# A two-layer graph network on one core: the setup rewritten around the edge records, and the pairs of tiles shifted by a place

## The chip, the cores and the metric

The kernel runs on one core of one Trainium2 chip. The metric is device time in microseconds (us), the median of several runs; "the profile" is one further execution recorded by the hardware profiler. The engines are TensorE (PE in the rows; PEld is its weight load), VectorE (DVE), ScalarE (ACT), GpSimd (POOL) and SyncE (SP), which only issues transfers. Transfers are issued by SP, ACT and POOL, each of which executes its program strictly in order.

## The reference, cut to what matters

```python
h = relu(layernorm(x))                                    # x: 1250 nodes x 512
weight = einsum('rb,bio->rio', w_comp, bases)             # 32 relations from 8 bases
msg = einsum('ni,rio->rno', h, weight)[etype, src] * edge_weight   # 40000 edges
x = x + segment_sum(msg, dst) + h_bias
h = relu(layernorm(x))
h = h @ W.T + b
row, col = edges and self loops; dis = rsqrt(degree)
x = x + relu(segment_sum(dis[row] * dis[col] * h[row], col))
```

The edges come sorted by destination (`dst`), and the low node numbers have far more of them than the high ones.

## The kernel before, in words

**Tiles and slots.** The nodes fall into 20 tiles of 64. Two tiles make a pair (ten pairs); `PAIR` says which, `PORDER` in which order the pairs are worked on. Each tile has a fixed number of slots of 128 edges, 335 in all. For every slot POOL gathers 128 rows of the table of normalised features (`rows_layer0`, 2,304 bytes a row) into one of eight buffers (`gath`, L766), and PE multiplies them with a one-hot matrix scaled by the edge's eight basis values (`sel`): twelve matmuls (L1614) sum the rows into the tile's accumulator, and one more (L1620) counts the edges by source for layer 1. L1620 is the last matmul of a slot, so its rows are the clock of the slots. DVE makes `sel` four slots at a time (L1194 to L1200).

**Ends of tiles.** When a tile's last slot is done, ACT and DVE split the accumulator into two halves of 16 bits (`flush`: ACT L874, DVE L1278, then the counts, DVE L1284 to L1287 and ACT L877). PE cannot begin the next tile's sums before that. When both tiles of a pair are done, 96 matmuls ("products", L1636) multiply them with the bases, which ACT and DVE have split likewise, one of eight bases at a time (`split_base`: ACT L885, DVE L1347). A planner (`place_products`) spreads the products over the slots behind; they are written into the order of PE. In the last stretch "partial" matmuls (L1643) of layer 1 take their place.

**Steps.** `STEPS[s]` lists what else each engine does at slot s: `flush`, `bsplit` (a base), `types`/`look` (the values of eight edge slots: one-hot of the relation by DVE L1140 from `types`, a matmul by PE L1514, the sum by DVE L1147, a cast by ACT L826), `largest`/`scale` (the scales of the bases and W, for which ACT must have squared all eight bases and W, L841).

**Setup.** SP loads the edge arrays and `x`; ACT packs source, destination, relation and weight of each edge into a record and writes the records to memory (L793 to L800). DVE and PE count the edges of each tile (L991, L1481, L1016 to L1024), which gives each slot its first edge. POOL then gathers the records slot by slot (`padr`, L738), and PE turns them so that an edge's fields stand in columns (L1496 to L1501); from these come `srcs`, the relations (`types_by_slot`, written out by SP L630 and loaded again by L624), and a `flag` that says whether the edges are in order. Meanwhile DVE takes the mean and variance of each 128 rows of `x` (L1008), ACT normalises them (L818) and casts them to the high half (L814), and the low half is made by POOL for seven of ten (L745) and by DVE for three (L1057). SP writes both halves into the table (L639). POOL waits for the whole table, the flag and `srcs` before the first gather; from the sixth gather on also for `s_cols`, which DVE gives when the column codes stand (L1180).

**What SP has in its queue**, in order: the identity blocks of the table (L607), a copy of `x` out of SBUF to `x_base` (L612), bases 0 to 4, the relations, the table, `types` 0 to 2, bases 5 to 7, the biases, W (L671), `types` 3 to 5, and two blocks of `x_base` back (L668).

## Time and profile before

| | before |
|---|---|
| median of 3 runs | 617.85 us (615.9 to 618.54) |
| the profiled execution | 612.81 us |
| its span, first to last instruction | 611.0 us |
| granted TensorE clock, mean | 0.909 |
| PE busy | 491.6 us of the span |
| POOL busy | 358.1 us |
| DVE busy | 347.5 us |
| ACT busy | 152.3 us |
| moved by the DMA engines | 132.32 MB |

A busy time is the sum of an engine's instructions; the granted clock is a share of full speed, and TensorE has two levels, 1.2 and 2.4 GHz (0.50 and 1.00 in the rows). The difference of 1.8 us between span and execution lies around the instructions.

### The profile page before, as it was taken

How to read it: one execution, taken by the hardware profiler on the slowest of the kernel's cores; microseconds unless marked ns; L12 is line 12 of the kernel's file. 1: busy time of each engine (PE TensorE's matmuls, PEld its weight loads, DVE VectorE, ACT ScalarE, POOL GpSimd, SP SyncE). 2: the span in 40 equal slices, each digit the busy share in tenths (PEclk: the TensorE clock that was granted, in tenths of full speed). 3: DMA queues.
4: the chain of work that ended last, by engine and by line, in shares of the span. 5: the costliest groups of instructions: out<-in, count | busy, mean ns of one | idle time of the engine just before them, and what ended most of it. 6: DMA issues, size and time to landing. Idle time of an engine off the chain costs nothing.

```text
span 611.0 us, 16039 instructions
## 1 busy us (share of the span) xinstructions
PE 491.6 (80%) x5902; PEld 313.8 (51%) x5902; DVE 347.5 (57%) x971; ACT 152.3 (25%) x272; POOL 358.1 (59%) x473
## 2 busy tenths in 40 slices
PE   3031446397999999999999999998999999989984
PEld 1021435265666666665565556555555565555531
DVE  7798137976575435755554754788646543332045
ACT  3392224552232011222220220320313202123010
POOL 3333626876676776775765757768747777760000
PEclk9655655699999999999999999998999999999986
DMA  8896965557786887795884867856867877773106
GB/s 281 295 351 225 392 187 145 160 160 201 221 273 202 243 271 225 215 277 176 251 254 144 273 208 221 273 179 189 268 178 212 255 238 237 239 231 107 33 11 162
DMA packets 53109, 132.32 MB, mean 217 GB/s; under 512 B 12109, under 2 KB 18110, under 8 KB 53030
## 3 DMA queue, kind: packets, MB, share of 16 engines
q0 software_dynamic: 27040, 99.60, 53.7%
q1 hardware_dynamic: 25036, 30.47, 16.0%
q8 instruction: 58, 0.95, 0.6%
q10 hardware_dynamic: 954, 1.13, 0.6%
q14 instruction: 21, 0.17, 0.1%
HBM read 120.32 MB, written 10.84 MB: 215 GB/s over the span
## 4 chain that ended last, share of the span: by engine, by line
PE 53%; DVE 13%; DMA 12%; issue 8%; ACT 5%; POOL 4%; SPq 3%; ACTq 1%; DVEq 0%
PE PS L1636 24%; PE PS L1614 17%; DMA gath<-rows_layer,srcs 7%; PE PS L1643 5%; PE PS L1684 4%; POOL gath L766 4%; DMA types<-types_by_slot 2%; SPq L624 2%; DVE room_b L1278 2%; ACT room_b L885 2%; DVE zt L1278 1%; DMA edge_records<-room_c 1%; DMA w1t<-edge_records,w1t 1%; DVE room_b L1347 1%; PE PS L1620 1%
## 5 line engine op out<-in xcount | busy, mean ns | idle before, releaser
L766 POOL DMA_INDIRECT gath<-rows_layer,srcs x335 | 341.8, 1020 | 168.8 <-issue 86.7
L1614 PE MATMUL PS<-sel,gath 128*128 128x48 f16 (+7 forms) x4020 | 315.7, 206 | 40.4 <-DVE zt L1278 12.1
L1614 PEld LDWEIGHTS PS<-sel,gath 128*128 128x128 f16 x4020 | 245.5, 102 | 164.6 <-issue 71.7
L1636 PE MATMUL PS<-room_b,zt 128*128 128x512 f16 x480 | 163.8, 385 | 1.4 <-DVE sel L1200 1.4
L1636 PE MATMUL PS<-room_b 128*128 128x512 f16 (+1 forms) x480 | 151.1, 380 | 0.9 <-DMA gath<-rows_layer,srcs 0.4
L1620 PE MATMUL PS<-oh_ad,gath 128*128 128x30 bf16 (+7 forms) x335 | 64.7, 193 | 0.0
L1194 DVE TENSOR_TENSOR masks<-iota_n,dloc 128x24 bf16<-128x24 f32 (+12 forms) x92 | 17.9, 195 | 80.9 <-issue 44.5
L1643 PE MATMUL PS<-u_t,room_c 128*128 128x512 f16 (+2 forms) x180 | 57.5, 404 | 3.7 <-issue 2.1
L1636 PEld LDWEIGHTS PS<-room_b 128*128 128x128 f16 (+1 forms) x480 | 47.3, 104 | 14.8 <-DVE room_b L1278 0.6
L826 ACT CAST val<-val_f 128x64 f16<-128x64 f32 x42 | 11.0, 261 | 168.4 <-DVE val_f L1151 163.4
L1636 PEld LDWEIGHTS PS<-room_b,zt 128*128 128x128 f16 x480 | 45.1, 99 | 5.9 <-issue 1.5
L1200 DVE TENSOR_TENSOR sel<-masks,val 128x192 f32<-128x192 bf16 (+12 forms) x92 | 38.8, 422 | 0.0
L1620 PEld LDWEIGHTS PS<-oh_ad,gath 128*128 128x128 bf16 x335 | 34.4, 103 | 3.1 <-issue 2.6
L1278 DVE SCALAR_TENSOR_TENSOR room_b<-PS,room_b 128x512 f16<-128x512 f32 x40 | 24.8, 683 | 13.5 <-ACT room_b L874 13.4
L1514 PE MATMUL PS<-wparts,oh_t 128*128 128x96 bf16 x84 | 10.8, 212 | 26.6 <-DVE oh_t L1140 24.6
L1278 DVE SCALAR_TENSOR_TENSOR zt<-PS,zt 128x512 f16<-128x512 f32 x40 | 24.8, 683 | 10.5 <-ACT zt L874 10.5
L1196 DVE TENSOR_TENSOR oh_ad<-iota_n,code 128x120 bf16<-128x120 f32 (+12 forms) x92 | 29.7, 323 | 0.0
L1147 DVE TENSOR_REDUCE val_f<-PS 128x64 f32<-128x192 f32 x42 | 14.9, 356 | 25.3 <-PE PS L1514 24.6
L1684 PE MATMUL PS<-w1t,hT_t 128*128 128x512 f16 (+1 forms) x120 | 27.5, 379 | 1.0 <-DVE val_f L1147 1.0
L877 ACT CAST room_c<-c_i 128x320 f16<-128x320 int32 (+1 forms) x40 | 16.1, 450 | 47.1 <-DVE c_i L1287 47.1
L1643 PEld LDWEIGHTS PS<-u_t,room_c 128*128 128x128 f16 (+2 forms) x180 | 18.4, 105 | 15.6 <-issue 8.1
L874 ACT ACTIVATE zt<-PS 128x512 f16<-128x512 f32 x40 | 20.6, 601 | 18.5 <-PE PS L1620 18.5
(227 smaller groups left out, 436.4 us busy)
## 6 DMA issues: line engine op xcount, KB each, us to landing
room_b<-in_L_gnn_bases_dram SPq DMA_DIRECT2D x8, 1024.0 KB, 9.9
gath<-rows_layer,srcs POOLq DMA_INDIRECT x335
types<-types_by_slot SPq DMA_DIRECT2D x168, 16.0 KB
x_t<-x_base SPq DMA_DIRECT2D x19, 128.0 KB, 5.0
u_t<-in_x_dram SPq DMA_DIRECT2D x9, 256.0 KB, 6.2
x_base<-u_t SPq DMA_DIRECT2D x9, 256.0 KB
x_layer<-x_t SPq DMA_DIRECT2D x16, 128.0 KB, 4.1
gath<-x_layer SPq DMA_DIRECT2D x16, 128.0 KB, 2.8
```

Source lines behind the costliest of these rows:

```text
L766: pool.indirect_dma_start(out=gath[:, s % UN, :], out_offset=None, in_=tab0_d[:, :], in_offset=bass.IndirectOffsetOnAxis(ap=srcs[:, s:s + ...
L874: a.activation(zt[q % 2][:, 0, f, :, TN * h:TN * (h + 1)], zbank(f), ACT.Copy, scale=ZDOWN).then_inc(s_hi, 1)
L877: a.copy(C[:, HA * k:HA * (k + 1), at:at + n], c_i[:, k, :].rearrange("p (a d) -> p a d", d=TN)[:, :, 0:n]).then_inc(s_cst, 1)
L1194: v.tensor_tensor(mask, iota_n[:, 0:w].unsqueeze(1).to_broadcast([P, k, w]), dloc[:, s:s + k].unsqueeze(2).to_broadcast([P, k, w]), ALU.is ...
L1196: v.tensor_tensor(oh_ad[:, there, 0:k, 0:HA * w], iota_n[:, 0:HA * w].unsqueeze(1).to_broadcast([P, k, HA * w]), code[:, s:s + k].unsqueez ...
L1200: v.tensor_tensor(sel[:, there, 0:k, 0:NB * w].rearrange("p k (b d) -> p k b d", b=NB), mask.unsqueeze(2).to_broadcast([P, k, NB, w]), val ...
L1278: v.scalar_tensor_tensor(lo, zbank(f), ZDOWN, hi, ALU.mult, ALU.subtract).then_inc(s_lo, 1)
L1614: mm(there, gath[:, s % UN, D * t + P * f:D * t + P * (f + 1)], sel_parts[:, here, k, 0:NB * w, u], start=first and t == 0 and u == 1, sto ...
L1620: mm(there, oh_r[:, s % UN, :], oh_ad[:, here, k, 0:HA * w], start=first, stop=True, skip_group_check=True).then_inc(s_used, 1)
L1636: last = mm(PS[0:r, PBANK[q], :], zt[q % 2][:, t, f, b, 0:r], base_hl[:, b, u, f, :], start=(m == 0), stop=(m == NM - 1))
L1643: return mm(PS[0:r, bank, :], there, u_part(i, t)[0:ROWS[i], :], start=start, stop=True, skip_group_check=not start)
L1684: last = mm(PS[0:r, MB, :], hT_t[:, s, f, 0:r], w1t[:, t, f, :], start=(f == s == t == 0), stop=(f == FT - 1 and s == 1))
```

## The change

It does these things.

- **Pairs.** `PAIR` is shifted by a place and `PORDER` is new: the first pair is now tiles 18 and 19 (9 and 5 slots; it was tiles 9 and 10 with 13 and 12), the last one tiles 0 and 17 (73 and 9; it was 0 and 19 with 73 and 5). The codes of the columns cost two more DVE instructions of 128x336. The bases are split at steps 9, 11, ... 23 (they were at 10, 13, ... 31), and the planner may place products from slot 24 on (it was 26). The identity blocks now come in four kinds instead of two (eight small DVE instructions instead of four, four writes instead of three).
- **SP.** The copy of `x` to `x_base` goes from memory to memory, in four transfers, behind the biases. The identity blocks wait for the record gather. `types` 3 to 5 stand right behind `types` 0 to 2. W is loaded again late, since the first load may be overwritten on another path.
- **ACT.** It issues bases 5 to 7 and a first load of W itself, behind the normalisation; it squares W before the first slot instead of at step 3. It normalises `x` in two groups of five.
- **POOL.** It makes no low halves any more; DVE makes all ten.
- **DVE.** It gives the standard deviation in two groups; behind the records it makes three low halves, then `srcs`, the checks and the flag, then the seven others, then the small table of `w_comp`.
- **PE.** The counting runs in four groups of five tiles (64 matmuls of 100 columns instead of 16 of 400), and the turned local index comes first.

```diff
-    PORDER = [5, 4, 6, 9, 3, 7, 2, 8, 1, 0]
-    PAIR = [(2 * p, NTI - 1 - 2 * p) for p in range(NT)]
+    PORDER = [9, 3, 4, 5, 6, 2, 7, 1, 8, 0]
+    TURN = NT - 2
+    PAIR = [(2 * p, 2 * ((TURN - p) % NT) + 1) for p in range(NT)]
...
-        SQ_SETUP, SC_AT, BS_AT, WT_AT = BEARLY, 7, 10, 38
+        SQ_SETUP, SC_AT, BS_AT, WT_AT = BEARLY, 7, 9, 38
...
-            STEPS[BS_AT + 3 * n].append(("bsplit", n))
+            STEPS[BS_AT + 2 * n].append(("bsplit", n))
...
-            GATHER, LAND, FREE, READY, RESERVE, FIRST = 5.8, 12.0, 14.0, 15.0, 14, 26
+            GATHER, LAND, FREE, READY, RESERVE, FIRST = 5.8, 12.0, 14.0, 15.0, 14, 24
...
-            for i in range(NT):
-                sp.wait_ge(s_xin[i], 16)
-                sp.dma_start(xbase_d[P * i:P * i + XROWS[i], :], x_in[0:XROWS[i], i, :]).then_inc(s_xbase, 16)
+            sp.wait_ge(s_rec_out, 48)
             load_base(0)
             sp.wait_ge(s_padr, 16 * C0)
+            sp.wait_ge(s_ident_fac, 2 * len(KINDS))
...
-            for v in range(1, TRING):
+            for v in range(1, TRING + VEARLY):
                 load_types(v)
-            for n in range(BEARLY, NB):
-                load_base(n)
...
+            for lo, hi in ((0, TN * HA), (TN * HA, P * HA), (P * HA, P * (NT - 2)), (P * (NT - 2), N)):
+                sp.dma_start(xbase_d[lo:hi, :], x[lo:hi, :]).then_inc(s_xbase, 16)
...
+            sp.wait_ge(s_sqb, SQ_SETUP + 1)
             sp.dma_start(w_in, W1.rearrange("(c p) i -> p c i", p=P)).then_inc(s_win, 16)
-            sp.wait_ge(s_xbase, 16 * NT)
-            for v in range(TRING, TRING + VEARLY):
-                load_types(v)
+            sp.wait_ge(s_xbase, 64)
             load_x(0)
             load_x(1)
...
-            for i in range(LOWS):
-                pool.wait_ge(s_h0hi, i + 1)
-                t = table_of(i)
-                g.tensor_tensor(t[:, 1, :], x_in[0:XROWS[i], i, :], t[:, 0, :], ALU.subtract).then_inc(s_h0lo_pool, 1)
...
+            for n in range(BEARLY, NB):
+                act.dma_start(base_in[:, n + 2, :, :], bases[n, :, :].rearrange("(f p) o -> p f o", p=P)).then_inc(s_bin[n], 16)
+            act.wait_ge(s_h0lo, FT)
+            act.dma_start(w_in, W1.rearrange("(c p) i -> p c i", p=P)).then_inc(s_win, 16)
             act.wait_ge(s_sqt, 1)
             for n in range(SQ_SETUP):
                 squares_of(n)
             for v in range(VEARLY):
                 val_hi(v)
+            squares_of(NB)
...
             for i in range(2, NT):
                 moments0(i)
+                if i == GROUP0:
+                    deviation(0)
...
-            pe.wait_ge(s_ohlt, NTI)
+            for r in range(0, NTI, CNT):
+                pe.wait_ge(s_ohlt, r + CNT)
+                for j in range(EC // 20):
+                    last = mm(PS[:, 0, 20 * r:20 * (r + CNT)], ones_b[0:EP, :], oh_lt[:, r:r + CNT, 20 * j:20 * (j + 1)],
+                              start=(j == 0), stop=(j == EC // 20 - 1))
```

How the order moves is seen at three places. First SP's queue from the last table write on, before; `room_b` holds the bases, `u_t` the rows of x and later W.

```order
L639 DMA rows_layer<-room_c 98x1024 [waits s_h0lo]
L624 DMA types<-types_by_slot 32x256 x8
L603 DMA room_b<-in_L_gnn_bases_dram 128x4x512 x3
L645 DMA hb_t<-in_L_gnn_h_bias_dram 128x512
L646 DMA b_t<-in_L_gnn_b_dram 128x512
...
L671 DMA u_t<-in_L_gnn_W_dram 128x4x512 [waits s_tab0]
L624 DMA types<-types_by_slot 32x256 [waits s_oht,s_xbase]
L624 DMA types<-types_by_slot 32x256 x3
```

The same stretch of SP's queue after the change.

```order
L645 DMA rows_layer<-room_c 98x1024 [waits s_h0lo]
L633 DMA types<-types_by_slot 32x256 x8
L633 DMA types<-types_by_slot 32x256 [waits s_oht]
L633 DMA types<-types_by_slot 32x256 x3
...
L649 DMA hb_t<-in_L_gnn_h_bias_dram 128x512
L650 DMA b_t<-in_L_gnn_b_dram 128x512
L652 DMA x_base<-in_x_dram 16x10240 x2
L652 DMA x_base<-in_x_dram 16x12288
L652 DMA x_base<-in_x_dram 16x7232
...
L678 DMA u_t<-in_L_gnn_W_dram 128x4x512 [waits s_sqb,s_tab0]
L674 DMA x_t<-x_base 64x512 [waits s_xbase]
```

The loads of `types` 3 (and, in the rows left out, 4 and 5) no longer stand behind the four loads of 1 MB, and the block of `x_base` that comes back stands behind a copy from memory to memory.

Second, DVE in the setup, before, from the sources (`srcs`) to the first scale (`bound`); `room_c` and `zt` hold the table's halves, `gath` is scratch here.

```order
L1102 CAST srcs<-PS 128x336 [waits s_tr]
...
L1125 COPY wtT<-PS 128x336 [waits s_tr,s_link]
...
L1130 TENSOR_SCALAR flag<-gath 1x1 [waits s_link]
L1057 TENSOR_TENSOR room_c<-u_t,room_c 128x512 [waits s_h0hi] x2
L1057 TENSOR_TENSOR room_c<-u_t,room_c 98x512 [waits s_h0hi]
L1112 TENSOR_SCALAR bound<-bound 128x1
```

The same part of DVE's order after the change.

```order
L1064 TENSOR_TENSOR zt<-u_t,zt 128x512 [waits s_h0hi] x3
L1100 COPY gath<-PS 128x336 [waits s_tr]
...
L1116 CAST srcs<-PS 128x336 [waits s_tr]
...
L1125 TENSOR_SCALAR flag<-gath 1x1 [waits s_link]
L1064 TENSOR_TENSOR zt<-u_t,zt 128x512 [waits s_h0hi] x2
L1064 TENSOR_TENSOR room_c<-u_t,room_c 128x512 [waits s_h0hi] x4
L1064 TENSOR_TENSOR room_c<-u_t,room_c 98x512 [waits s_h0hi]
L1130 TENSOR_SCALAR zt<-zt 128x1
```

DVE has ten low halves instead of three, three of them ahead of `srcs` and seven behind the flag.

Third, DVE at the end of the first tile, before: the scales (`unscale_x` is their last), a base (`room_b<-room_b,scale_i`), the flush (`zt<-PS,zt`).

```order
L1341 TENSOR_SCALAR unscale_x<-unscale_i 128x1 [waits s_link]
L1140 TENSOR_SCALAR oh_t<-types,rel 128x256 [waits s_look,s_types1,s_scaled]
L1347 SCALAR_TENSOR_TENSOR room_b<-room_b,scale_i 128x2048 [waits s_bhi]
L1194 TENSOR_TENSOR masks<-iota_n,dloc 128x4x11 [waits s_sel,s_used,s_val]
L1196 TENSOR_TENSOR oh_ad<-iota_n,code 128x4x55
L1200 TENSOR_TENSOR sel<-masks,val 128x4x88 [waits s_mask]
L1278 SCALAR_TENSOR_TENSOR zt<-PS,zt 128x8x64 [waits s_hi] x4
```

The same place after the change, from the first tile's flush to the second tile's.

```order
L1310 SCALAR_TENSOR_TENSOR zt<-PS,zt 128x8x64 [waits s_hi] x4
...
L1374 TENSOR_SCALAR unscale_x<-unscale_i 128x1 [waits s_link]
L1380 SCALAR_TENSOR_TENSOR room_b<-room_b,scale_i 128x2048 [waits s_bhi,s_scaled]
L1169 TENSOR_SCALAR oh_t<-types,rel 128x256 [waits s_look,s_types1]
L1327 TENSOR_TENSOR room_c<-room_c,ident 128x64 [waits s_cst]
L1333 TENSOR_REDUCE deg_p<-room_c 128x10 [waits s_own]
L1335 TENSOR_TENSOR deg<-deg,deg_p 128x10 [waits s_degp]
L1380 SCALAR_TENSOR_TENSOR room_b<-room_b,scale_i 128x2048 [waits s_bhi]
...
L1310 SCALAR_TENSOR_TENSOR zt<-PS,zt 128x8x64 [waits s_hi] x4
```

The first flush now stands ahead of the scales, and two bases stand ahead of the second one, which ends a tile of five slots.

## Rows read from the trace of the kernel before

**Rows 1.** The page, busy time of each engine: us, share, instructions.

```profile
PE 491.6 (80%) x5902; PEld 313.8 (51%) x5902; DVE 347.5 (57%) x971; ACT 152.3 (25%) x272; POOL 358.1 (59%) x473
```

**Rows 2.** Busy time by stretch; last: granted clock, DMA share, GB/s.

```profile
57.00:78.00 21.00, 6.48 (x91) 6.19 (x91) 5.89 (x20) 6.27 (x7) 13.13 (x13) 0.58 1.03 387
72.10:84.98 12.88, 0.00 (x0) 0.03 (x1) 0.43 (x4) 3.17 (x3) 1.89 (x2) 0.56 0.95 294
86.00:140.00 54.00, 36.84 (x458) 27.99 (x456) 43.36 (x90) 23.98 (x28) 40.37 (x29) 0.70 0.54 154
500.00:545.00 45.00, 41.71 (x620) 26.31 (x619) 13.59 (x49) 7.21 (x13) 34.11 (x36) 1.00 0.79 238
```

**Rows 3.** Chain that ended last, in order of time: start, length, what.

```profile
11.19 7.42 DMA edge_records<-room_c
...
21.55 7.31 DMA w1t<-edge_records,w1t
...
60.53 7.05 SPq L624
...
69.94 14.58 DMA types<-types_by_slot
...
538.82 4.60 DMA gath<-rows_layer,srcs
...
558.71 20.92 PE PS L1636 x96
```

**Rows 4.** Timeline of POOL: start, length, line, idle before.

```profile
28.23 6.04 POOL L745 TENSOR_TENSOR zt<-u_t,zt 128x512 f16<-128x512 f32 x5 [5.73 <-ACT zt L814]
...
54.59 0.96 POOL L766 DMA_INDIRECT gath<-rows_layer,srcs  x1 [17.87 <-issue]
...
61.37 1.04 POOL L766 DMA_INDIRECT gath<-rows_layer,srcs  x1 [0.30 <-issue]
...
93.60 2.69 POOL L766 DMA_INDIRECT gath<-rows_layer,srcs  x1 [0.30 <-issue]
```

**Rows 5.** Timeline of DVE in the setup.

```profile
28.95 0.46 DVE L1043 COPY w1t<-w1t 128x3 f32<-128x3 f32 x1 [2.61 <-DMA w1t<-edge_records,w1t]
...
29.51 1.12 DVE L1045 TENSOR_SCALAR w1t<-w1t 128x3 f32<-128x3 f32 x1
30.66 0.16 DVE L1046 TENSOR_TENSOR w1t<-w1t 128x3 f32<-128x3 f32 x1
...
33.10 3.75 DVE L1050 TENSOR_SCALAR w1t<-w1t 128x128 f32<-128x128 f32 x3
...
48.58 1.87 DVE L1057 TENSOR_TENSOR room_c<-u_t,room_c 128x512 f16<-128x512 f32 x3
...
60.72 0.20 DVE L1194 TENSOR_TENSOR masks<-iota_n,dloc 128x40 bf16<-128x40 f32 x1
```

**Rows 6.** Timeline of SP: transfers issued.

```profile
10.49 9.10 SPq L612 DMA_DIRECT2D x_base<-u_t  x10
```

**Rows 7.** Timeline of PE: first slot, then ends of slots 24, 28, 48, 252, 334.

```profile
64.61 0.98 PE L1614 MATMUL PS<-sel,gath 128*128 128x80 f16 x12 [7.76 <-issue]
...
113.22 0.26 PE L1620 MATMUL PS<-oh_ad,gath 128*128 128x55 bf16 x1
...
125.41 0.19 PE L1620 MATMUL PS<-oh_ad,gath 128*128 128x50 bf16 x1
...
156.17 0.20 PE L1620 MATMUL PS<-oh_ad,gath 128*128 128x55 bf16 x1
...
446.04 0.20 PE L1620 MATMUL PS<-oh_ad,gath 128*128 128x65 bf16 x1
...
554.92 0.20 PE L1620 MATMUL PS<-oh_ad,gath 128*128 128x65 bf16 x1
```

**Rows 8.** Waits of PE up to 145 us: total, times, longest.

```profile
PE PS L1514 <- DVE oh_t L1140: 24.6, 5, 12.9
```

**Rows 9.** DVE's half of the split of a base, all eight.

```profile
L1347 DVE SCALAR_TENSOR_TENSOR room_b<-room_b,scale_i x8: 2344/2350/2352, 93.1 to 133.1; 128x2048 f16<-128x2048 f32 x8
```

More of the change, by code:

```diff
@@ L229, in gnn_kernel @@
         gap_max = take_g(f32, SL)[0:1, :]
-        assert all(TROWS[i] == TN for i in TORDER[:-1])
         rec = rec_w[0:EP, :].rearrange("p (c k) -> p c k", k=4)
@@ L1027, in _ @@
                 moments0(i)
+                if i == GROUP0:
+                    deviation(0)
             v.memset(stats[:, :], 0.0).then_inc(s_stat0, 1)
@@ L1074, in _ @@
             v.reduce_sum(viol_s, viol, AX.X)
+            low(0)
+            low(1)
+            low(2)
+            dve.wait_ge(s_tr, 1)
+            link(v.tensor_copy(dloc_f, PS[:, 1, 0:SLV]))
+            link(v.tensor_tensor(valid, dloc_f, win_c, ALU.is_lt))
+            link(v.reduce_sum(have, valid[:, 0:SL], AX.X))
+            v.tensor_scalar(have, have, -float(E) / P, None, ALU.add).then_inc(s_have, 1)
+            dve.wait_ge(s_slotmm, 1)
+            link(v.tensor_copy(row_f, PS[0:1, PB, 0:SLP]))
+            v.tensor_tensor(same[:, 0:NSAME], row_f[:, REP:SL], row_f[:, 0:NSAME], ALU.is_equal)
+            begin = PS[0:1, CB, 0:SL + 1]
+            dve.wait_ge(s_gap, 1)
+            v.tensor_copy(hops[:, SL:SL + 1], begin[:, 0:1])
+            link(v.tensor_tensor(hops[:, 0:SL], begin[:, 1:SL + 1], gap_max, ALU.subtract))
+            link(v.tensor_tensor(hops[:, 0:SL], hops[:, 0:SL], begin[:, 0:SL], ALU.is_gt))
+            v.reduce_sum(bad, same[:, 0:NSAME + SL + 1], AX.X).then_inc(s_have, 1)
+            dve.wait_ge(s_tr, 2)
+            v.tensor_copy(srcs[:, :], PS[:, 2, 0:SLV]).then_inc(s_srcs, 1)
+            begins = PS[0:1, CB, 0:SLP].rearrange("p (g k) -> p g k", k=WPACK)
+            link(v.tensor_copy(pack_f, begins[:, :, WPACK - 1]))
+            for k in reversed(range(WPACK - 1)):
+                there = pack_f if k else slots[0:1, :]
+                link(v.scalar_tensor_tensor(there, pack_f, float(1 << WBITS), begins[:, :, k], ALU.mult, ALU.add))
+            dve.wait_ge(s_okmm, 1)
+            link(v.tensor_scalar(ok3, PS[:, 0, 0:3], 0.0, None, ALU.is_equal))
+            link(v.tensor_reduce(ok, ok3, AX.X, ALU.min))
+            v.tensor_scalar(flag[0:1, :], ok[0:1, :], -1.0, 1.0, ALU.mult, ALU.add).then_inc(s_flag, 1)
+            for i in range(3, NT):
+                low(i)
+            link(v.tensor_scalar(blk_i, part_i, R.bit_length() - 1, None, ALU.logical_shift_right))
+            link(v.tensor_copy(blk, blk_i))
             link(v.scalar_tensor_tensor(rel[:, :], blk, -float(R), part_f[:, :], ALU.mult, ALU.add))
@@ L1126, in _ @@
             link(v.tensor_tensor(bound[:, SC_V:SC_V + 1], sq_max[:, :], sq_max[:, :], ALU.mult))
-            dve.wait_ge(s_okmm, 1)
-            link(v.tensor_scalar(ok3, PS[:, 0, 0:3], 0.0, None, ALU.is_equal))
-            link(v.tensor_reduce(ok, ok3, AX.X, ALU.min))
-            v.tensor_scalar(flag[0:1, :], ok[0:1, :], -1.0, 1.0, ALU.mult, ALU.add).then_inc(s_flag, 1)
-            for i in range(LOWS, NT):
-                low(i)
             powers(SC_V, SC_V + 1)
@@ L1493, in _ @@
             columns_of(0)
-            pe.wait_ge(s_loc, 2 * C0)
+            pe.wait_ge(s_loc, C0)
+            for c in range(C0):
+                last = tr(PS[:, 1, P * c:P * (c + 1)], padr[:, c, :, 1], ident[:, :])
+            last.then_inc(s_tr, 1)
             for c in range(C0):
```

149 lines of the change are left out of this document (74 added, 75 removed).

## The prediction

> **What bounds the kernel now.** I read the busy times first. PE is busy for 491.6 of 611.0 us and no other engine comes near [rows 1], so PE bounds the kernel as a whole; what it does not work, it waits, and where it waits is read from the chain that ended last and from the ends of the slots. The first slot begins at 64.61 us [rows 7]: the setup is a tenth of the time, and PE has almost nothing to do in it. From 72.10 to 84.98 PE does nothing at all [rows 2]. The longest wait of PE up to 145 us, 12.9 us, is for the one-hot of the relations [rows 8], and the chain says why: SP stood 7.05 us in the issue of a `types` load and the load then took 14.58 us to land [rows 3]. It stood behind three bases and W, 4 MB, in SP's own queue, while the DMA engines were full (share 1.03, 387 GB/s from 57 to 78 us [rows 2]). From 86 to 140 us DVE is the engine that sets the pace, 43.36 of 54.00 us busy against PE's 36.84, at a mean granted clock of 0.70 [rows 2]. After that PE is nearly always busy, until the last stretch: from 500 to 545 us POOL makes 36 gathers, one per 1.25 us (45.00 / 36), and PE follows them [rows 2]. The chain ends with 96 products in 20.92 us, 0.218 us each [rows 3].
>
> **The setup, step by step.** Without the `x_base` copy, which SP issued from 10.49 to 19.6 us [rows 6], the writing of the records (7.42 us) and their gather (7.31 us) [rows 3] have the DMA engines almost to themselves; the nearest undisturbed transfer takes 4.60 us to land [rows 3], so the records can be there between 23 us and the present 28.86. It makes little difference: DVE stood waiting only 2.61 us for them, so it was free at 26.34 [rows 5]. The extra identity blocks fall into its wait for the counting, and the second half of the deviation may cost it 0.3 us: it begins at about 26.6 instead of 28.95.
>
> Then comes the part that POOL slows. While POOL subtracts (28.23 on, seven instructions [rows 4]), DVE's 128x3 instructions take 1.12 us, and 0.16 us where they miss one; the three of 128x128 take 3.75 us [rows 5]. Seven such instructions would take about 2.5 us instead of 8: with POOL's share gone, the columns and relations are out 8 us earlier, at about 29.2. This pays for the work that DVE takes over: seven low halves at 0.62 us (1.87 / 3 [rows 5]) are 4.4 us, three of ten ahead of `srcs`, the rest behind the flag. The last low half then ends at about 43.6, where now it ends at 50.45 [rows 5]; SP writes the table until 45 to 46, now beside bases 5 to 7 and W on ACT's queue. At 387 GB/s [rows 2] these 4.2 MB are 10.8 us of the DMA engines, of which the table may meet half. First gather: 47 at best, 54.6 as now [rows 4] at worst; I take 50.5. DVE's chain to the first `masks`, now at 60.72 [rows 5], gains 4 us in scales and low halves and loses about 1 for the two new code instructions and 1 for `types` 1, which land behind the table: 58 to 60. PE began 3 to 4 us behind `masks` [rows 5, 7]; I take 60.5 for the first slot instead of 64.6: **-4.1** (bounds 0 and -8).
>
> **The hole.** `types` 3 is issued right behind `types` 2, at about 49 us, on a queue without the 1 MB loads. Even 14.58 us to land [rows 3] would bring it at 64, before slot 6 needs it (60.5 plus 7 slots of 1.07 us, from 64.61 to 72.10 [rows 2, 7], is 68). **-12.9.**
>
> **What is late next.** Slots 7 to 28 took from 84.98 to 125.60 [rows 2, 7], 40.6 us, paced by DVE. The same DVE work waits there now, closer together: the second tile has five slots, so its flush comes behind the scales and two bases of 2.35 us [rows 9] (each behind ACT's half), and `look` 5 at slot 22 behind three more. Queued behind these on DVE are the selections and the flush that PE needs. At best the stretch keeps its 40.6 us; at worst it takes 5.9 us more, since now all eight bases have to be split before the flush at slot 28, where five or six of them had been (2.5 x 2.35). The wait behind two bases at slot 13 is the nearest thing, but PE has slots in hand at slot 22; I take **+1.9**. Slot 28 then ends at 110.5: 125.6 - 4.1 - 12.9 + 1.9.
>
> **From slot 28 to 48.** 30.8 us now (125.60 to 156.37 [rows 7]). Counted in the order, PE has 82 products there instead of 57: 25 x 0.218 = +5.5. The bases that are done by then no longer stand in DVE's way (up to -5.9); I take half: **+2.5**.
>
> **From slot 48 to 252.** The same 13 tile ends and 655 products instead of 657; the columns of the edges up to slot 252 are the same in sum, counted from the windows: **0**. The other order of the tiles changes which slots are narrow, not their sum; I allow 4 us to both sides.
>
> **From slot 252 to 334.** 108.9 us now (446.24 to 555.12 [rows 7]). 29 products are no longer in it, 6.3 us where PE bounds, nothing where POOL's 1.25 us a gather do. More than half of it is of the second kind [rows 2]: **-1.9**. The tail behind slot 334 is the same work: 96 products, the last partial sums, the output.
>
> **Sum.** -4.1 - 12.9 + 1.9 + 2.5 - 1.9 = -14.5. The profiled execution took 612.81 us (span 611.0); it would take 598.3. The median of the runs is 617.85, 5 us above the profiled one; from it the forecast is 603.4 us.
>
> **The rivals.**
>
> *The gathers are held up* (10%). Between 80 and 112 us the eight bases fill DVE for 18.8 us. A gather that met a base took 2.69 us instead of 0.95 [rows 4], 1.74 us more; if each base costs PE that much, 14 us are lost. Against it speaks that the eight buffers hide a single late gather, and that 29 gathers in 54 us lost only 0.44 us each to it (40.37 / 29 - 0.95 [rows 2]). Half of the 14 gives -7.5: 610 us. The Trainium skill (SBUF — State Buffer, section "SBUF: two separate sides") says that DVE and GpSimd share a pair of ports as an exclusive lock, held for the whole instruction, the loser fully blocked. By that rule every base blocks POOL for its full length and the sum would be near -7.5 or less; the rows on POOL's subtractions bear the lock out, those on the gathers only in part.
>
> *The hole stays* (5%). The change would not do what it says if `types` 3 were late for another reason than SP's queue, say because the DMA engines are as full as before: the copy of `x` (2.56 MB), the second W and the biases now run from 55 to 70. The 12.9 us stay and the gain is 1.6: 616 us. Against it: SP itself stood still for 7.05 us [rows 3], which only its own queue explains. The Trainium skill (Trainium Kernel Development and Optimization, section "Key Constraints") says that issuing from several engines saves only the sequencer's issue time, since all queues run on the same 16 DMA engines. By it the move of four loads to ACT's queue would be worth the 7.05 us of issue and not the landing, and the sum would be about -8; no row of the kernel before shows two queues with large loads at once.
>
> *Slower* (5%). `types` 6, which DVE needs at slot 25 (about 105 us), now stands in SP's queue behind the first block of `x_base`, and that behind a copy from memory to memory of which the trace shows no example. The nearest row issues 2.5 MB in 9.1 us [rows 6]; issued at 56 it would be there before 75. If the copy ran at a sixth of 387 GB/s and landed at 95, nothing would be lost; from about 97 on each us is one of PE's, and beyond 112 the kernel is slower than before. Landing at 120: 626 us.
>
> *More than forecast* (5%): the start at -8 and the last stretch at -6.3, 594 us.
>
> **Chances and range.** The forecast, a gain of 8 to 20 us, holds 75%; the four rivals 25%. A difference within 0.5%, 3.1 us, is about what a measurement of this kernel cannot tell from none. Faster: the forecast, the held gathers, the larger gain: 0.89; the same: 0.06; slower: 0.05. The range of 596 to 612 reaches from the larger gain into the held gathers.
>
> **What would show it.** Right: the first slot at 59 to 62 us; DVE's instructions of 128x3 at 0.2 us throughout; no wait of PE above 8 us behind the first slot; a wait at slot 14 for DVE (flush behind two bases) of 4 to 8 us; slot 28 at 108 to 113; slot 252 at 430 to 437; the stretch from 500 us on paced by gathers of 1.25 us. Wrong: a first gather that still waits until 54 us, PE waiting for `types` or for ACT's squares at slots 6 and 7, or an SP that stands at the second block of `x_base`.

## The result, and the profile after

| | before | after |
|---|---|---|
| median, same chip | 616.88 us (614.38 to 618.54, 4 runs) | 627.98 us (627.2 to 630.05, 4 runs) |
| ratio to before | | 1.021 (95% interval 1.0174 to 1.0246) |
| the profiled execution, its span | 612.81, 611.0 us | 627.2, 625.4 us |
| PE busy | 491.6 us | 488.8 us |

The change makes the kernel 2.1% slower; forecast were 603.4 us and a gain. (Ratios here and below are taken over undisturbed runs alone, so they are not quite those of the medians, here 1.018.) The two profiled executions stand 14.4 us apart, the medians 11.1: the one of before was faster than any of its four timed runs, so the distances to before by slot, which are read from the traces, may be some 3 us too large. The page of the changed kernel first, busy time of each engine, answering to [rows 1].

```profile
PE 488.8 (78%) x5954; PEld 313.2 (50%) x5954; DVE 347.3 (56%) x989; ACT 153.0 (24%) x273; POOL 353.5 (57%) x466
```

PE works 2.8 us less in a span that is 14.4 us longer: PE waits 17.2 us more. The question is where. The timeline of PE after, first slot and ends of slots 7, 28, 48, 252 and 334, answers to [rows 7]; L1657 is now the last matmul of a slot.

```profile
67.37 1.30 PE L1651 MATMUL PS<-sel,gath 128*128 128x104 f16 x12 [6.87 <-DVE sel L1231]
...
81.82 0.20 PE L1657 MATMUL PS<-oh_ad,gath 128*128 128x65 bf16 x1
...
124.60 0.20 PE L1657 MATMUL PS<-oh_ad,gath 128*128 128x45 bf16 x1
...
164.98 0.19 PE L1657 MATMUL PS<-oh_ad,gath 128*128 128x50 bf16 x1
...
463.78 0.19 PE L1657 MATMUL PS<-oh_ad,gath 128*128 128x60 bf16 x1
...
569.67 0.20 PE L1657 MATMUL PS<-oh_ad,gath 128*128 128x65 bf16 x1
```

The first slot begins 2.8 us later than before, behind a wait of 6.87 us that the profile puts down to DVE's `sel`. From slot 7 to 13 the change is ahead (82.0 against 86.3 at slot 7, by 4.3 us); at slot 28 it is ahead by 0.8, at 48 behind by 8.8, at 252 by 17.8, at the last slot by 14.8.

**The setup** got what was hoped for on DVE and lost it in the transfers. DVE's timeline after: an instruction of 128x3, the local indices, `srcs`, the last low halves.

```profile
26.05 0.17 DVE L1081 TENSOR_SCALAR w1t<-w1t 128x3 f32<-128x3 f32 x1
...
26.85 0.83 DVE L1086 TENSOR_SCALAR w1t<-w1t 128x128 f32<-128x128 f32 x3
...
35.84 0.48 DVE L1116 CAST srcs<-PS 128x336 uint32<-128x336 f32 x1
...
39.01 3.08 DVE L1064 TENSOR_TENSOR room_c<-u_t,room_c 128x512 f16<-128x512 f32 x5
```

The three instructions of 128x128 take 0.83 us where they took 3.75 [rows 5], and the last low half ends at 42.1 instead of 50.45. Now the chain that ended last, in this stretch, and the busy times by stretch (sum, then engines, granted clock, DMA share, GB/s).

```profile
31.50 12.95 DMA types_by_slot<-h_t
44.47 0.32 SPq L633
...
48.71 0.48 SPq L645
...
50.65 7.00 DMA types<-types_by_slot
...
65.48 13.12 DMA gath<-rows_layer,srcs
```

```profile
28.00:40.00 12.00, 6.31 (x29) 4.15 (x28) 11.52 (x31) 6.29 (x10) 0.00 (x0) 0.64 1.03 384
40.00:57.00 17.00, 0.32 (x2) 0.14 (x2) 7.81 (x33) 9.30 (x11) 0.00 (x0) 0.50 1.04 390
57.00:69.00 12.00, 2.26 (x23) 1.91 (x24) 9.41 (x31) 6.32 (x8) 7.71 (x8) 0.50 0.70 217
69.00:83.00 14.00, 8.27 (x105) 7.49 (x102) 2.69 (x11) 2.36 (x5) 7.02 (x9) 0.69 0.97 357
```

From 28 to 57 us the DMA engines are full: 29 us at 384 to 390 GB/s are 11.2 MB, seven bases and W (8 MB) among them. The 96 KB of relations, which SP issued behind bases 1 to 4 in its own queue, take 12.95 us to land. SP waits for them before it goes on to `types` 0 and the last six table writes (L645), so the last of these is issued at 48.71, 6.6 us behind the last low half. Then the sixth gather takes 13.12 us, beside the copy to `x_base` and the second W: a new hole where the old one was. `types` 1, issued behind the table at 50.65, landed 7.00 us later, and DVE's chain to the first `masks` (65.26) starts there. POOL's first and sixth gather, which stood at 54.59 and 61.37 [rows 4]:

```profile
58.62 0.95 POOL L766 DMA_INDIRECT gath<-rows_layer,srcs  x1 [37.44 <-issue]
...
65.48 1.15 POOL L766 DMA_INDIRECT gath<-rows_layer,srcs  x1 [0.84 <-DVE code L1211]
```

**Behind the setup**, from slot 8 to 29, PE has three long waits for DVE: for the flush at slot 13, for the one-hot of `look` 5 at slot 22, and for the flush at slot 28.

```profile
99.80 0.78 PE L1651 MATMUL PS<-sel,gath 128*128 128x72 f16 x6 [8.13 <-DVE zt L1310]
...
116.42 0.32 PE L1551 MATMUL PS<-wparts,oh_t 128*128 128x96 bf16 x2 [7.47 <-DVE oh_t L1169]
...
129.22 0.42 PE L1651 MATMUL PS<-sel,gath 128*128 128x88 f16 x3 [3.10 <-DVE room_b L1310]
```

The wait for the same look in the kernel before:

```profile
111.08 0.32 PE L1514 MATMUL PS<-wparts,oh_t 128*128 128x96 bf16 x2 [3.81 <-DVE oh_t L1140]
```

### The profile page after: what moved, and what is told of

It reads as the page before. It is cut to its first block, busy times and chain, and to the rows that moved or that the text cites. A ratio compares the mean times of both kernels' runs of the same rounds, so it can differ in the third digit from the quotient of the medians.

```text
span 625.4 us, 16152 instructions
## 1 busy us (share of the span) xinstructions
PE 488.8 (78%) x5954; PEld 313.2 (50%) x5954; DVE 347.3 (56%) x989; ACT 153.0 (24%) x273; POOL 353.5 (57%) x466
## 4 chain that ended last, share of the span: by engine, by line
PE 51%; DMA 17%; DVE 14%; issue 7%; ACT 4%; POOL 3%; SPq 2%; DVEq 0%; ACTq 0%; POOLq 0%
PE PS L1673 24%; PE PS L1651 17%; DMA gath<-rows_layer,srcs 13%; PE PS L1721 5%; PE PS L1680 4%; POOL gath L766 3%; DVE zt L1310 2%; DMA types_by_slot<-h_t 2%; ACT room_b L896 1%; DVE room_b L1380 1%; DMA types<-types_by_slot 1%; DVE room_b L1310 1%; PE PS L1657 1%; ACT zt L885 1%; DVE sel L1231 1%
## 5 line engine op out<-in xcount | busy, mean ns | idle before, releaser
L1673 PE MATMUL PS<-room_b,zt 128*128 128x512 f16 (+1 forms) x480 | 164.6, 387 | 1.1 <-DMA gath<-rows_layer,srcs 0.6
L1673 PE MATMUL PS<-room_b 128*128 128x512 f16 x480 | 150.7, 380 | 0.6 <-DMA gath<-rows_layer,srcs 0.6
L1657 PE MATMUL PS<-oh_ad,gath 128*128 128x30 bf16 (+7 forms) x335 | 64.3, 192 | 0.1
L1225 DVE TENSOR_TENSOR masks<-iota_n,dloc 128x24 bf16<-128x24 f32 (+12 forms) x92 | 17.8, 194 | 78.9 <-issue 45.2
L1680 PE MATMUL PS<-u_t,room_c 128*128 128x512 f16 (+1 forms) x180 | 55.6, 380 | 4.9 <-issue 3.3
L1673 PEld LDWEIGHTS PS<-room_b 128*128 128x128 f16 x480 | 44.7, 98 | 16.8 <-DMA gath<-rows_layer,srcs 0.7
L1673 PEld LDWEIGHTS PS<-room_b,zt 128*128 128x128 f16 (+1 forms) x480 | 48.0, 106 | 5.7 <-DMA gath<-rows_layer,srcs 0.7
L1657 PEld LDWEIGHTS PS<-oh_ad,gath 128*128 128x128 bf16 x335 | 34.0, 102 | 3.2 <-issue 2.2
L1551 PE MATMUL PS<-wparts,oh_t 128*128 128x96 bf16 x84 | 10.7, 210 | 31.6 <-DVE oh_t L1169 30.1
L1721 PE MATMUL PS<-w1t,hT_t 128*128 128x512 f16 (+1 forms) x120 | 29.7, 401 | 4.6 <-DVE val_f L1176 4.4
L885 ACT ACTIVATE room_b<-PS 128x512 f16<-128x512 f32 x40 | 20.6, 602 | 31.9 <-PE PS L1657 29.3
```

Source lines behind the costliest of these rows:

```text
L885: a.activation(zt[q % 2][:, 0, f, :, TN * h:TN * (h + 1)], zbank(f), ACT.Copy, scale=ZDOWN).then_inc(s_hi, 1)
L1225: v.tensor_tensor(mask, iota_n[:, 0:w].unsqueeze(1).to_broadcast([P, k, w]), dloc[:, s:s + k].unsqueeze(2).to_broadcast([P, k, w]), ALU.is ...
L1657: mm(there, oh_r[:, s % UN, :], oh_ad[:, here, k, 0:HA * w], start=first, stop=True, skip_group_check=True).then_inc(s_used, 1)
L1673: last = mm(PS[0:r, PBANK[q], :], zt[q % 2][:, t, f, b, 0:r], base_hl[:, b, u, f, :], start=(m == 0), stop=(m == NM - 1))
L1680: return mm(PS[0:r, bank, :], there, u_part(i, t)[0:ROWS[i], :], start=start, stop=True, skip_group_check=not start)
L1721: last = mm(PS[0:r, MB, :], hT_t[:, s, f, 0:r], w1t[:, t, f, :], start=(f == s == t == 0), stop=(f == FT - 1 and s == 1))
```

## The experiments

Two theories stood against each other for the loss: **the setup** (its transfers), and **the pairs** (tile ends, base splits and products lie elsewhere). All times of before in these runs are 614.6 to 615.2 us; ratios are to before on the same chip. Ends of slots, in us, read from each trace as above:

| slot | before | after | 1: old pairs | 2: new pairs alone | 4: copy late | 7: short pair fourth | 8: 1 and 4 | 10: splits late |
|---|---|---|---|---|---|---|---|---|
| 0 | 65.6 | 68.7 | 67.6 | 66.7 | 68.2 | 68.0 | 67.5 | 69.5 |
| 7 | 86.3 | 82.0 | 82.2 | 86.2 | 73.8 | 82.7 | 73.5 | 82.9 |
| 14 | 100.7 | 102.0 | 96.2 | 106.5 | 94.0 | 92.8 | 87.8 | 96.6 |
| 29 | 126.8 | 133.1 | 122.1 | 138.4 | 125.2 | 120.1 | 117.1 | 131.5 |
| 48 | 156.4 | 165.2 | 151.9 | 172.0 | 157.3 | 159.2 | 147.1 | 163.6 |
| 104 | 228.6 | 245.2 | 223.8 | 252.5 | 237.4 | 248.6 | 220.4 | 243.6 |
| 144 | 289.6 | 310.1 | 285.2 | 316.8 | 302.0 | 313.2 | 283.5 | 308.5 |
| 252 | 446.2 | 464.0 | 442.1 | 470.7 | 456.2 | 466.3 | 440.4 | 463.4 |
| 334 | 555.1 | 569.9 | 550.6 | 576.2 | 564.6 | 573.5 | 549.6 | 570.9 |

**1. The new setup with the old pairs.**

```diff
-    PORDER = [9, 3, 4, 5, 6, 2, 7, 1, 8, 0]
-    TURN = NT - 2
+    PORDER = [5, 4, 6, 9, 3, 7, 2, 8, 1, 0]
+    TURN = NT - 1
...
+        SQ_SETUP, SC_AT, BS_AT, WT_AT = BEARLY, 7, 10, 38
+            STEPS[BS_AT + 3 * n].append(("bsplit", n))
```

> The new setup with the old pairs, the old steps of the base splits (10, 13, 16, ...), the old first slot of products (26) and the old step of the histogram's preparation. Theory A (the loss is made by the pairs: products drawn 31 ahead at slot 48, flushes and splits closer together on DVE): the first slot ends near 68.7 us as in the changed kernel, slot 7 near 82 (4 ahead of before), and that lead is kept to the end: 610 to 614 us. Rival B (the loss is made by the setup's DMA traffic): the same late gathers and nothing won later: 624 to 628 us.

609.8 us, ratio 0.9925 (0.990 to 0.9949): a gain of 0.75%. It is 4.1 us ahead at slot 7 and 4.5 at the last slot. Theory A holds.

**2. The old setup with the new pairs**, the same lines the other way round.

> The old setup with the new pairs and all that goes with them (four kinds of identity, the split steps 9, 11, 13, ..., first product slot 24). Theory A (pairs cost): the hole at 74 to 87 us stays, and slots 8 to 48 cost some 10 us more on top: 626 to 632 us. Rival B (setup costs): about the time of before, 615 to 619 us.

635.96 us, ratio 1.0353 (1.0309 to 1.0398). Level with before at slot 7, 5.8 us behind at 14, 15.6 at 48, 27.2 at 144, 21.1 at the end. The pairs cost more than the 10 us of theory A. The setup is worth a gain, the pairs a loss some four times as large.

**3. The relations ahead of the identities and bases 1 to 4.**

```diff
+            sp.wait_ge(s_loc, 2 * C0)
+            for c in range(C0):
+                sp.dma_start(types_d[P * c:P * (c + 1), :], typ16[:, c, :]).then_inc(s_typd, 16)
             sp.wait_ge(s_ident_fac, 2 * len(KINDS))
```

> The changed kernel, with the three writes of the type rows issued ahead of the identities and of bases 1 to 4 on SP. Theory A (the type rows wait for the bases in SP's DMA queue and the table writes stand behind that on SP): the write lands in about 5 us instead of 13, types 0 near 44 instead of 51, the first gather is issued near 54 instead of 58.6, the first slot ends near 64, and the time falls by 3 to 5 us to 623 to 625. Rival B (the DMA engines are full until 56 us whatever the order): the write lands sooner but the table later or as late, first gather 57 to 59, time 626 to 629.

632.99 us, ratio 1.0297 (1.025 to 1.0344), slower than both theories said. Transfers of the two kernels, after and then here: issue, KB each, median us to landing.

```profile
types_by_slot<-h_t SPq DMA_DIRECT2D x3, 32.0 KB, 13.0
```

```profile
types_by_slot<-h_t SPq DMA_DIRECT2D x3, 32.0 KB, 1.6
```

The relations land in 1.6 us instead of 13.0, so it was the loads ahead of them. (In the changed kernel base 4 lands at 42.07 and the first of the relations at 42.80, which speaks for their place in SP's queue; but here they were issued while no other load was under way, so full engines are not ruled out.) But now the identities and bases are issued 5.7 us later (the bases from 31.64 instead of 25.90), the table's writes stand behind them, and the first gather comes at 64.32 instead of 58.62. The 96 KB themselves are not what delays the rest: SP now stands until DVE has the relations (it issues them at 28.25) before it goes on to identities and bases. A wait moved ahead in a queue delays all that is behind it.

**4. The copy to `x_base` and the second W later.** The copy, W and the first two loads of `x` back move from ahead of slot 0 to step 25 of SP's list.

```diff
+            for s in range(VEND):
+                if s == 25:
+                    with sp.If(any_order < 1):
+                        for lo, hi in ((0, TN * HA), (TN * HA, P * HA), (P * HA, P * (NT - 2)), (P * (NT - 2), N)):
+                            sp.dma_start(xbase_d[lo:hi, :], x[lo:hi, :]).then_inc(s_xbase, 16)
...
+                    load_x(0)
+                    load_x(1)
```

> The changed kernel, with the copy of x to x_base, the second load of W and the first two loads of x issued at step 25 of SP's list (behind the load of type rows 8) instead of ahead of slot 0. Theory A (the sixth gather took 13.1 us because the copy and the weight were in the queues beside it): gathers 6 to 8 land in 4 to 6 us, slot 4 ends near 73 instead of 78, and 3 to 5 us stay to the end: 623 to 625. Rival B (DVE's chain of looks and selections is late at slots 5 to 14 anyway, so an earlier gather only waits): slot 4 earlier, slot 14 as before, 626 to 629. Rival C (the moved copy now meets the gathers of slots 20 to 28): 629 to 633.

621.02 us, ratio 1.0107 (1.006 to 1.0153). Slot 4 ends at 71.6 instead of 78.2, slot 7 at 73.8 instead of 82.0, and 8 us of it stay until slot 252, 5.3 to the last. The busy times by stretch of this run show why:

```profile
69.00:83.00 14.00, 12.03 (x159) 10.56 (x157) 9.39 (x36) 6.17 (x10) 10.58 (x12) 0.74 0.83 245
```

PE does 12.03 us of work from 69 to 83 where the changed kernel did 8.27, and the DMA engines are no longer full. Theory A holds, with more than it asked for. Which of the copy, W and the loads back counts most was not separated.

**5 and 6. The products cut, with the new and with the old pairs.** After the first of each pair, a product takes 64 columns instead of 512.

```diff
-                    last = mm(PS[0:r, PBANK[q], :], zt[q % 2][:, t, f, b, 0:r], base_hl[:, b, u, f, :], start=(m == 0), stop=(m == NM - 1))
+                    w = D if m == 0 else 64
+                    last = mm(PS[0:r, PBANK[q], 0:w], zt[q % 2][:, t, f, b, 0:r], base_hl[:, b, u, f, 0:w], start=(m == 0), stop=(m == NM - 1))
```

> The changed kernel with every product but the first of each pair cut from 512 to 64 columns (left out: 7/8 of the products' computation). It is to be read against the same cut on the new setup with the old pairs. Theory P (the pairs cost by the order of the products: 31 to 60 more are drawn by slots 48 to 144 than with the old pairs, where PE is the bound, and they are missing as filler later, where the gathers are): with the products nearly free, the distance between the two kernels falls from 17.5 us to 8 or less by the last slot. Rival F (the pairs cost by DVE's flushes, splits and looks, which stand closer together): the distance stays at 15 to 20 us, as the waits for DVE don't depend on the products.

> The new setup with the old pairs, and the same cut of the products to 64 columns (left out: 7/8 of the products' computation). Theory P: 8 us or less faster than the cut kernel with the new pairs. Rival F: 15 to 20 us faster than it.

583.94 and 572.71 us: 11.2 us apart (17.5 with whole products, 2.85% of 615). In the traces the two stand 10.7 us apart at slot 29 and 10.8 at the last. With whole products it was 11.1 and 19.3. So the 8.2 us that the pairs lose behind slot 29 go with the products, and the 11 ahead of it don't. Neither theory alone: the loss has two halves. (From slot 29 on the granted clock of the two cut kernels was 0.81 and 0.82, of the whole ones 0.99 and 1.00, so the cut ones are compared with each other alone.)

Both halves are seen in the busy times by slots. Old pairs on the new setup, slots 9 to 14, 49 to 84, 185 to 252:

```profile
82.93:96.24 13.31, 6.24 (x83) 4.82 (x84) 10.59 (x32) 4.98 (x8) 8.31 (x7) 0.73 0.84 259
...
151.94:200.07 48.13, 45.88 (x604) 29.80 (x603) 28.96 (x85) 11.30 (x25) 33.32 (x36) 1.00 0.77 233
...
341.37:442.10 100.73, 92.76 (x1233) 59.96 (x1232) 65.40 (x187) 18.32 (x41) 72.92 (x70) 0.98 0.75 223
```

The changed kernel, the same slots:

```profile
83.08:102.02 18.94, 7.92 (x82) 6.23 (x82) 16.27 (x42) 8.72 (x12) 8.32 (x7) 0.72 0.68 202
...
165.17:218.24 53.07, 51.66 (x631) 32.85 (x629) 32.80 (x92) 12.88 (x28) 35.84 (x37) 1.00 0.78 230
...
365.11:463.97 98.86, 86.67 (x1216) 56.44 (x1213) 58.87 (x170) 14.03 (x32) 72.70 (x68) 1.00 0.75 219
```

In slots 9 to 14 DVE has 16.27 us to do instead of 10.59 (two flushes and two splits where the old pairs have one of each; the scales stand in both), and the stretch is 5.6 us longer. From slot 49 to 84 PE has 5.8 us more to do (23 products more, 5.0 us at 0.218) and the stretch is 4.9 us longer. From 185 to 252 it has 6.1 us less to do, and the stretch is only 1.9 us shorter: with fewer products PE waits there, 12.2 instead of 8.0 us. (17 products fewer are 3.7 of the 6.1 us; what else is in it, run 1's granted clock of 0.98 or the width of the slots, was not separated.) From the end of slot 29 to the last, the changed kernel and then run 1:

```profile
133.10:569.90 436.80, 398.00 (x5247) 256.36 (x5244) 230.52 (x673) 84.20 (x181) 297.98 (x298) 0.99 0.74 218
```

```profile
122.10:550.60 428.50, 400.36 (x5259) 256.07 (x5257) 239.66 (x690) 88.83 (x188) 297.91 (x300) 1.00 0.75 223
```

With the new pairs PE has no more work in sum, 398.0 us against 400.4, but it waits 38.8 us against 28.1. Work brought forward is paid almost in full where PE is full and given back only in part where it filled waits.

**7. The short pair fourth instead of first**, with the split steps of before.

```diff
-    PORDER = [9, 3, 4, 5, 6, 2, 7, 1, 8, 0]
+    PORDER = [3, 4, 5, 9, 6, 2, 7, 1, 8, 0]
```

> The changed kernel with the same new pairs, but the short one (9 + 5 slots) worked fourth instead of first, so that the first pair has 26 slots; base splits and first product slot at their old steps. From slot 104 on the products lie as in the changed kernel. Theory S (the short pair ahead puts two uncovered flushes and eight splits into slots 8 to 28): slots 8 to 48 as with the old pairs, so some 9 to 13 us come back and the time is 614 to 619 us. Rival M (the shifted pairs cost by their later tiles, whatever comes first): 623 to 628 us.

631.31 us, ratio 1.0257 (1.0202 to 1.0313). Up to slot 29 the loss is gone (120.1 against 122.1 with the old pairs), as theory S has it; but from slot 29 to 104, where the short pair now lies, 128.5 us pass against 101.7. Theory S is wrong in the sum: what is won ahead of slot 29 is lost where the pair of 14 slots now lies. That pair brings the same two flushes and 96 products as one of 24. In the order 282 products lie from slot 30 to 104, with the old pairs 223; the 59 more are 12.9 us at 0.218, about half of the loss there. The other half was not separated.

**8. Old pairs and the late copy together**, the edits of 1 and 4.

> The new setup with the old pairs, and the copy of x to x_base, the second load of W and the first loads of x issued at step 25 of SP's list. Theory (the two effects add: the late gathers of slots 3 to 6 are the setup's, the rest is the pairs'): 609.8 less 5 to 8 us, 602 to 605 us. Rival (the old pairs' first tile of 13 slots waits for a look or a flush that hides the earlier gathers): 607 to 610 us.

606.17 us, ratio 0.9861 (0.9822 to 0.9899), better than both kernels by 1.4% and 3.4%. Between the two expectations: 8.7 us won at slot 7 shrink to 1.0 at the last, and to 3.6 in the median (the trace of run 1 is of its fastest execution, 607.71 us).

**9. Old pairs, with each pair's products due 26 slots sooner.**

```diff
-                    due = LAST[2 * q + 4] - 3 if q < Q7 else HL + 8 if q == Q7 else HL + 36
+                    due = LAST[2 * q + 4] - 29 if q < Q7 else HL + 8 if q == Q7 else HL + 36
```

> The new setup with the old pairs, and the planner told that each pair's products are due 26 slots sooner, so that they lie nearly where the changed kernel has them (96 by slot 48, 232 by 84, 419 by 144, 748 by 252; the old pairs have 77, 175, 370 and 723, the changed kernel 96, 230, 430 and 763). Theory P (products drawn early cost where PE is full and are missing later): 609.8 plus 6 to 10 us, 616 to 620, with up to 12 us lost by slot 144 and less than half of it given back. Rival F (where the products lie costs nothing; the flushes cost): lost by slot 144 and given back by the last slot, 608 to 612 us.

659.98 us, ratio 1.0742 (1.0702 to 1.0783): far beyond theory P's 620. Counted in the traces, the products by slots 48, 84, 144 and 252 are 96, 228, 412 and 747 here, 94, 227, 428 and 749 in the changed kernel and 63, 173, 368 and 720 with the old pairs in their order, so the edit does bring them where it was meant to, though the counts expected for the two others were too high. Waits of PE from slot 29 to the last, here and then in the changed kernel: total, times, longest.

```profile
PE PS L1651 <- DVE room_b L1310: 19.4, 19, 4.3
PE PS L1651 <- DVE zt L1310: 11.8, 13, 5.7
```

```profile
PE PS L1651 <- DMA gath<-rows_layer,srcs: 17.6, 25, 1.9
PE PS L1721 <- DVE val_f L1176: 4.4, 1, 4.4
...
PE PS L1651 <- DVE zt L1310: 1.8, 6, 0.4
PE PS L1651 <- DVE room_b L1310: 1.8, 5, 0.6
```

Here the products are used up before a tile ends, so flushes stand bare: 31.2 us against 3.6. (In 10 of the 16 tile ends from slot 37 to 256 the order has no product in the slot behind the flush.) In the changed kernel there are 14 behind each of these flushes; its pairs are ready sooner too. So 9 shows that early products cost, by another way than in the changed kernel, and says nothing of how much they cost there; that rests on 5 and 6.

**10. The new pairs, with the splits at slots 14 to 26.**

```diff
-            STEPS[BS_AT + 2 * n].append(("bsplit", n))
+            STEPS[(14, 16, 18, 20, 22, 24, 25, 26)[n]].append(("bsplit", n))
```

> The changed kernel, with the eight base splits at slots 14, 16, 18, 20, 22, 24, 25 and 26 instead of 9, 11, ..., 23: none stands between the first two flushes. Theory C (the two splits ahead of the second flush make slots 8 to 14 long): these take about 14 instead of 18.9 us, slots 14 to 28 up to 3 us more, and the time falls by 2 to 5 us to 623 to 626. Rival (the second flush itself and its selection cost it): slots 8 to 14 at 17 to 19 us and the time 627 to 630.

628.26 us, ratio 1.0221 (1.0175 to 1.0266): no change. Slots 9 to 14 take 12.9 us instead of 18.9, as theory C has it, but slot 29 alone takes 17.1 instead of 8.3. The longest wait of PE there:

```profile
PE PS L1651 <- DVE room_b L1310: 11.9, 1, 11.9
```

The third tile's flush writes into `room_b` and must follow all eight splits; with the new pairs it stands at slot 28 instead of 37. The work was only moved along, to the next place with a due time.

**11 and 12. Old pairs, late copy, and bases 5 to 7 (run 11) or 1 to 4 (run 12) loaded behind.** In both the scales come at step 13 and the splits from 15 on; 11 issues bases 5 to 7 behind ACT's third look, 12 this:

```diff
             for v in range(1, TRING + VEARLY):
                 load_types(v)
+                if v == 2:
+                    for n in range(1, BEARLY):
+                        load_base(n)
```

> The version with the new setup, the old pairs and the copy of x moved behind, with bases 5 to 7 (3 MB) loaded behind the third look instead of ahead of the table's writes; their squares then at slots 8 to 10, the scales at 13 and the splits from 15. Theory (what holds the table's last write is the 11 MB in the DMA queues from 28 to 57 us, of which these are 3): the first gather is issued 5 to 8 us sooner, near 51, and the time is 600 to 604 us. Rival (the order of SP's issues and ACT's halves set the first gather, not the bytes): first gather as before within 2 us and 605 to 609 us; or the later loads meet the first gathers and cost what was won.

> The version with the new setup, the old pairs and the copy of x moved behind, with bases 1 to 4 (4 MB) issued by SP behind the table's writes and types 0 to 2 instead of ahead of them; their squares follow the first three looks, the scales are at 13 and the splits from 15. Theory (the type rows and the table's writes stand behind these 4 MB in SP's DMA queue): the type rows land in 2 to 5 us, the first gather is issued 6 to 10 us sooner (48 to 52) and the time is 598 to 603 us. Rival (the 4 MB then stand beside the first gathers): first gather sooner, but slots 0 to 7 take 8 us longer, 604 to 609 us.

Run 11: ratio 0.9858 (0.9795 to 0.992); its runs lie wide apart, from 603.8 us up, and its trace is of one of 612.75. Run 12: 605.76 us, ratio 0.9855 (0.982 to 0.989). Both are level with 8. The first gathers, in 11 and then in 12:

```profile
50.52 0.99 POOL L770 DMA_INDIRECT gath<-rows_layer,srcs  x1 [29.97 <-issue]
```

```profile
51.49 1.00 POOL L771 DMA_INDIRECT gath<-rows_layer,srcs  x1 [30.59 <-issue]
```

7 to 8 us sooner than the 58.36 of run 8: the bytes do set the first gather. But the moved bases land late, and the scales and the first flush wait for them. The chain of 11, then of 12:

```profile
55.78 28.28 DMA room_b<-in_L_gnn_bases_dram
...
84.08 2.00 ACT val L851 x2
```

```profile
48.94 21.80 DMA room_b<-in_L_gnn_bases_dram
70.77 2.01 ACT val L852 x2
```

Slot 13 ends at 89.9 and 86.6, against 86.7 in run 8. In both runs the scales stand at step 13, and all of these bytes are needed before it; their order only chose who waited.

**13 and 14. Seven of the eight splits cut as well**, with the new and the old pairs, from 5 and 6.

```diff
+                w = 64 if n else D
...
-                v.scalar_tensor_tensor(base_hl[:, n, 1, :, :], base_in[:, n + 2, :, :], scale[:, SC_BASE:SC_BASE + 1],
+                v.scalar_tensor_tensor(base_hl[:, n, 1, :, 0:w], base_in[:, n + 2, :, 0:w], scale[:, SC_BASE:SC_BASE + 1],
```

> The changed kernel with the products cut to 64 columns as before, and seven of the eight base splits cut to 64 of 512 columns on ACT and DVE (left out: 7/8 of the products' and of these splits' computation). To be read against the next run at slot 29, where the two kernels stood 10.7 us apart (132.5 and 121.8) with whole splits. Theory D (the splits, 2.35 us each on DVE and 2.0 on ACT, now in slots 9 to 28 instead of 10 to 37, hold the selections and flushes up): slot 29 ends near 118 to 121 and the distance is 4 us or less. Rival (the third flush in these slots costs it by itself): slot 29 ends near 126 and the distance stays at 7 to 11 us.

> The new setup with the old pairs, and the same cuts of products and splits (left out: 7/8 of the products' computation and of that of seven splits). Theory D: slot 29 ends near 115 to 117, 5 us or so sooner than with whole splits, 4 us or less ahead of the cut kernel with the new pairs. Rival: near 117, 7 to 11 us ahead of it.

568.44 and 560.53 us, 7.9 apart. Slot 29 ends at 118.8 and 112.7: 6.1 us apart, where it was 10.7. Between the two expectations: the splits make 4.6 us of the 10.7. Of the other 6.1, 1.5 were there at slot 0, it is 4.8 at slot 14 (behind the second flush), 3.3 at slot 28, and slot 29 (behind the third) adds 2.8. That a flush more in these slots is the cause was not tested by itself. At the last slot the traces stand 11.8 us apart, the medians 7.9, so how much of the splits' part is left at the end stays open (by the medians of 5, 6, 13 and 14 it is 3.3 us, 11.2 less 7.9).

## Why the prediction was wrong, step by step

Forecast and measured, profiled execution against profiled execution:

| step | forecast | measured |
|---|---|---|
| start (first slot's end) | -4.1 | +3.1 |
| the hole (slots 1 to 7) | -12.9 | -7.4 |
| what is late next (slots 8 to 28) | +1.9 | +3.5 |
| slots 29 to 48 | +2.5 | +9.6 |
| slots 49 to 252 | 0 | +9.0 |
| slots 253 to 334 | -1.9 | -3.0 |
| sum | -14.5 | +14.8 |

**Start.** DVE's part was right: 128x3 at 0.15 to 0.17 us, last low half at 42.1 (forecast 43.6). Wrong was the sentence that "the table may meet half" of the 10.8 us of bases 5 to 7 and W. It left out bases 1 to 4 and the relations, which stand ahead of the table on SP. The first gather came 8.1 us behind the forecast of 50.5; with 3 or 4 MB taken out of the way it came at 50.5 and 51.5 (runs 11 and 12). Two queues moved hardly more than one: 384 to 390 GB/s from SP's and ACT's loads together, 373 from SP's alone, in the kernel before (the 387 of [rows 2] are SP's loads and POOL's gathers together):

```profile
31.00:45.00 14.00, 5.37 (x23) 3.64 (x23) 13.35 (x33) 13.72 (x20) 5.46 (x5) 0.58 1.01 373
```

That is what the Trainium skill says (Trainium Kernel Development and Optimization, section "Key Constraints"): several issuing engines share the same 16 DMA engines. The first slot hung on DVE's chain too: its first `masks` were forecast for 58 to 60 us, with 1 us for `types` 1 "behind the table", and came at 65.26, since `types` 1 landed at 57.65; the first `sel` was done 1.1 us ahead of the first slot.

**The hole.** The step reasoned on `types` 3 alone, and that wait did go. It forgot that the copy, moved out of the early setup, and the second W would meet the gathers of slots 3 to 7; the sixth took 13.12 us. Without them the stretch takes 5.6 us (run 4, 68.2 to 73.8). The rival "the hole stays" named the same transfers, but as what delays `types` 3. The block of `x_base` behind the copy, the rival "slower", held nothing up.

**What is late next.** The sum was off by only 1.6 us, in part by luck. The wait that was forecast came, 8.1 us for the flush at slot 13, behind two splits; but PE's waits for flushes in these slots are no longer than before in sum (10.3 against 11.1 us). What differs is `look` 5 at slot 22, where the prediction had "slots in hand": PE waits 7.47 us for it, 3.81 before. The rival "gathers held up" is not what differs: gathers that met a split took up to 3.60 us in the changed kernel, and up to 3.73 with the old pairs.

**Slots 29 to 48.** The 5.5 us of products were counted rightly. The deduction for splits that "no longer stand in DVE's way" was not there to be had. Left out of this step was the flush at slot 28, behind the last split: two tile ends now lie in the stretch instead of one, and slot 29 alone takes 8.3 us against 1.2, with 14 products and PE's wait of 3.10 us in it. Over the stretch PE is busy 6.9 us more, at a granted clock of 0.96 instead of 1.00, and waits 2.7 us more. Before, and then after:

```profile
125.60:156.37 30.77, 26.10 (x340) 18.02 (x338) 21.37 (x50) 8.44 (x15) 22.96 (x20) 1.00 0.65 182
```

```profile
124.80:165.17 40.37, 32.97 (x366) 21.96 (x365) 22.93 (x60) 9.36 (x20) 22.88 (x23) 0.96 0.58 167
```

**Slots 49 to 252.** This is the step that weighs most. It reasoned that as many products and as many tile ends give the same time. In sum there are as many, but they lie 32 to 78 ahead of the old order between slots 65 and 144, and 29 ahead at 252. With the products cut, the new and the old pairs differ by 1.8 us from slot 48 to 252 (279.4 and 277.6); with whole ones by 8.6 (298.8 and 290.2).

**Slots 253 to 334.** Right in kind: 29 products fewer gave back 3.0 of 6.3 us (forecast 1.9), since gathers pace PE there [rows 2].

In all, from runs 1 and 2: the new setup is worth -4.8 us, the new pairs +17.5 on it and +21.4 on the old one. Of the 19.3 by slots (traces of after and of run 1's fastest execution), 8 go with the products and, up to slot 29, 4.6 with the splits; some 6 are left, which may be the third flush ahead of slot 30 and are not settled. The forecast asked what the setup's waits were worth, and took the order of the tiles as free.
